# Attention and routing kernel: TensorE's fillers between the score products in another order

## The reference

```python
xl = _layer_norm(x, ln_l_g, ln_l_b);  xg = _layer_norm(x, ln_g_g, ln_g_b)
# x is (32, 256, 128), 16 heads of 8
...   # local: _mha over blocks of the first axis: all 32 rows see each other, per position
...   # glb: one _mha of xg with itself over the same 32 rows
return local + glb
...
x = _layernorm(x + attention(x))
logits = tokens @ Wg                      # 8 experts, capacity T / E
idx = jnp.argmax(gates, axis=1)           # one expert per token, places counted in token order
hidden = jax.nn.relu(jnp.einsum('ech,ehf->ecf', expert_in, W1) + b1[:, None, :])
expert_out = jnp.einsum('ecf,efh->ech', hidden, W2) + b2[:, None, :]
x = _layernorm(x + out)
```

## Time and profile before

| | us |
|---|---|
| median of 3 runs | 732.38 |
| lowest, highest | 731.19, 732.99 |
| span of the profiled execution | 731.2 |
| units 8 to 29, by GpSimd's step (168.00 to 486.48) | 318.5 |

### The profile page before, as it was taken

How to read it: one execution, slowest core, us unless ns; L and a number is a source line. 1 busy time by engine, 2 the same in 40 slices (tenths; PEclk the granted TensorE clock), 3 DMA queues, 4 the chain that set the end, 5 groups by cost and what they waited for, 6 DMA issues and landing times.

```text
span 731.2 us, 19237 instructions
## 1 busy us (share of the span) xinstructions
PE 637.1 (87%) x6502; PEld 358.2 (49%) x6502; DVE 549.3 (75%) x1652; ACT 489.6 (67%) x1108; POOL 488.8 (67%) x972
## 2 busy tenths in 40 slices
PE   0569698899999999999999999999999359999990
PEld 0435443454445444544555554455444237677770
DVE  5565596889998998899999998988993205666663
ACT  1425475887988888889888888898888233444430
POOL 4133333568888788888888887886776714667676
PEclk9857898999999999999999999999999569999996
DMA  5585589897576675575666765655631022333410
GB/s 111 142 169 110 145 202 174 211 179 211 154 138 170 161 128 148 129 167 158 120 168 162 140 156 151 129 152 111 155 64 36 24 64 81 98 107 99 123 47 32
DMA packets 144001, 95.53 MB, mean 131 GB/s; under 512 B 12052, under 2 KB 136173, under 8 KB 143904
## 3 DMA queue, kind: packets, MB, share of 16 engines
q1 hardware_dynamic: 138048, 85.54, 50.1%
q0 software_dynamic: 4096, 7.81, 3.8%
q10 hardware_dynamic: 1760, 0.96, 0.6%
HBM read 47.70 MB, written 45.74 MB: 128 GB/s over the span
## 4 chain that ended last, share of the span: by engine, by line
PE 49%; DVE 18%; DMA 9%; issue 8%; POOL 7%; SPq 6%; ACT 3%; POOLq 0%; ACTq 0%; DVEq 0%
DVE mx L940 10%; PE ps_o L555 10%; PE ps_b L528 7%; PE ps_a L1372 6%; PE ps_a L510 4%; PE ps_b L1366 3%; DMA ks<-k_stack 3%; DMA qs<-mT 3%; PE ps_m L586 2%; PE ps_f L476 2%; POOL out L1486 2%; PE ps_f L466 2%; PE ps_m L599 2%; SPq L326 2%; PE ps_f L471 2%
## 5 line engine op out<-in xcount | busy, mean ns | idle before, releaser
L940 DVE TENSOR_REDUCE mx<-ps_a 128x2 f32<-128x512 f32 (+1 forms) x576 | 359.9, 651 | 61.5 <-PE ps_a L510 59.6
L762 ACT ACTIVATE prob<-ps_b 128x512 f32<-128x512 f32 (+1 forms) x576 | 298.7, 572 | 75.8 <-PE ps_b L528 74.3
L528 PE MATMUL ps_b<-qs,ks 59*128 59x256 bf16 (+1 forms) x1152 | 192.5, 271 | 14.0 <-DMA qs<-mT 6.3
L510 PE MATMUL ps_a<-ks,qs 56*128 56x256 bf16 (+1 forms) x1152 | 190.0, 275 | 14.7 <-DMA ks<-k_stack 12.7
L555 PE MATMUL ps_o<-prob,vp 128*32 128x256 f32 (+1 forms) x2304 | 172.8, 384 | 0.4 <-ACT prob L762 0.4
L528 PEld LDWEIGHTS ps_b<-qs,ks 59*128 59x128 bf16 x1152 | 80.9, 96 | 106.7 <-ACT prob L762 52.0
L510 PEld LDWEIGHTS ps_a<-ks,qs 56*128 56x128 bf16 x1152 | 75.9, 96 | 27.8 <-DMA ks<-k_stack 14.4
L1486 POOL DMA_INDIRECT out<-res,dest x64 | 65.4, 1022 | 34.2 <-DVE res L1461 19.1
L1225 POOL DMA_INDIRECT routed<-row,slot x64 | 67.2, 1050 | 29.8 <-issue 26.3
L555 PEld LDWEIGHTS ps_o<-prob,vp 128*32 128x32 f32 x2304 | 49.8, 110 | 58.2 <-issue 50.2
L1159 POOL CAST mpart<-mx 128x16 bf16<-128x16 f32 x72 | 14.0, 195 | 70.8 <-DVE mx L940 60.0
(11 more groups left out here) (130 smaller groups left out, 1041.7 us busy)
## 6 DMA issues: line engine op xcount, KB each, us to landing
qs<-q_stack SPq DMA_DIRECT2D x72, 192.0 KB
ks<-k_stack SPq DMA_DIRECT2D x72, 192.0 KB
q_stack<-part SPq DMA_DIRECT2D x18, 384.0 KB
k_stack<-part SPq DMA_DIRECT2D x18, 384.0 KB
q_stack<-part SPq DMA_DIRECT2D x18, 256.0 KB
k_stack<-part SPq DMA_DIRECT2D x18, 256.0 KB
routed<-empty SPq DMA_DIRECT2D x8, 520.0 KB, 8.3
rows_sb<-routed SPq DMA_DIRECT2D x16, 260.0 KB, 3.7
```

What stands on the lines that cost most here:

```text
L510: ins = nc.tensor.matmul(ps_a[:, n % 3, qt * S:qt * S + keys.stop - keys.start], qs[half, b, hp, qt * P:(qt + 1) * P], ks[half, b, hp, key ...
L528: ins = nc.tensor.matmul(ps_b[:, 1 - e, kt * n:(kt + 1) * n], ks[half, u % 3, hp, kt * P:(kt + 1) * P], qs[half, u % 3, hp, queries], star ...
L762: nc.scalar.activation(prob[:, hp, half * n:(half + 1) * n], ps_b[:, half, 0:n], ACT.Exp).then_inc(exp_done, 1)
L940: nc.vector.reduce_max(mx[:, u % 2, :, col], ps_a[:, n % 3].rearrange("p (t k) -> p t k", t=2)[:, :, 0:k], axis=AX).then_inc(max_done, 1)
```

## The change

TensorE's fillers are dealt out anew: a value product does both key halves in one go (`values(u, q)`, eight products in a row) and these stand alone in slots 1, 3, 5 and 7; everything else stands in slots 0, 2, 4 and 6. Waits move with what they guard. The other engines' orders are fitted to it. The counts of the routing move to the last 24 columns of `ps_m`, so that they don't share columns with the turned maxima. The orders of GpSimd and SyncE stay as they are, row by row.

```diff
+        def values(u, q):
+            if there(u):
+                p_v(u, q, 0)
+                p_v(u, q, 1)
 
         def fill(u, hp):
             if hp == 0:
-                if there(u - 1):
-                    p_v(u - 1, 3, 0)
                 if there(u):
                     pe.wait_ge(mT_ready, 2 * u + 1)
...
                     turn_max(u, 1)
-            if hp == 1:
-                if there(u - 1):
-                    p_v(u - 1, 3, 1)
-                if routes(u - 3):
...
-                    count_tokens(u - 3)
                 if first is not None:
                     turn_x(first, 0)
                     turn_x(first, 1)
+                if second is not None:
+                    project_in(second, "k", 0)
+                    project_in(second, "k", 1)
+            if hp == 1:
+                values(u - 1, 3)
             if hp == 2:
+                if there(u):
+                    pe.wait_ge(mT_ready, 2 * u + 2)
...
+                if routes(u - 3):
+                    count_tokens(u - 3)
+                if first is not None:
+                    project_in(first, "q", 0)
                 if second is not None:
                     project_in(second, "v", 0)
-                    project_in(second, "v", 1)
...
                     turn_o(u - 1)
             if hp == 3:
-                if there(u):
-                    p_v(u, 0, 0)
+                values(u, 0)
+            if hp == 4:
+                if there(u - 1):
+                    pe.wait_ge(o_normed, u)
...
                 if there(u + 1):
...
                     turn_max(u + 1, 0)
                 if first is not None:
-                    project_in(first, "q", 0)
-            if hp == 4:
-                if there(u):
-                    p_v(u, 0, 1)
...
+                    project_in(first, "q", 1)
+                if second is not None:
+                    project_in(second, "v", 1)
+                if there(u + 1) and there(u - 1):
                     pe.wait_ge(mT_ready, 2 * u + 3)
...
+                if routes(u - 2):
+                    turn_x1(u - 2)
                 if there(u - 1):
                     turn_oN(u - 1)
...
             if hp == 5:
-                if there(u):
-                    p_v(u, 1, 0)
+                values(u, 1)
+            if hp == 6:
                 if routes(u - 2):
                     logits(u - 2)
                 if there(u - 1):
                     project(u - 1)
-            if hp == 6 and there(u):
-                p_v(u, 1, 1)
-                p_v(u, 2, 0)
             if hp == 7:
-                if there(u):
-                    p_v(u, 2, 1)
-                if first is not None:
-                    project_in(first, "k", 0)
-                    project_in(first, "k", 1)
+                values(u, 2)
...
         # ScalarE, step(u)
             if there(u):
-                exponential(u, 4)
+                exponential(u, 4, (0,))
+            if there(u + 1):
+                copy_max(u + 1, 0)
+            if there(u):
+                exponential(u, 4, (1,))
             if there(u - 1) or routes(u - 2):
                 copy_turned(u)
             if first is not None:
                 first_part_q(first)
             if second is not None:
+                place_v(second, 0)
                 place_v(second, 1)
...
         # VectorE, fill(u, hp, e)
             if at == (0, 0) and routes(u - 3):
-                top_priority(u - 3)
-            if at == (0, 1) and routes(u - 3):
+                priorities(u - 3)
+            if at == (0, 1):
+                if routes(u - 2):
+                    mean_variance(u - 2)
+                if routes(u - 3):
+                    top_priority(u - 3)
...
-            if at == (6, 1):
+            if at == (7, 0):
                 if there(u - 1):
                     add_residual(u - 1)
                 if routes(u - 2):
                     logit_max(u - 2)
-            if at == (7, 0):
+            if at == (7, 1):
                 if routes(u - 2):
                     shift_logits(u - 2)
                 if routes(u - 1):
                     statistics(u - 1)
-            if at == (7, 1):
-                if routes(u - 2):
-                    priorities(u - 2)
-                if routes(u - 1):
-                    mean_variance(u - 1)
```

More of the change, by code:

```diff
@@ L605, in count_tokens @@
             pe.wait_ge(mask_ready, batch(u) + 1)
-            nc.tensor.matmul(ps_m[:, 0:2 * E], c["tri_bf"][:], mask[:].rearrange("p t e -> p (t e)"), start=True, stop=False)
-            nc.tensor.matmul(ps_m[:, E:2 * E], c["ones_bf"][:], mask[:, 0], start=False, stop=True)
-            nc.tensor.matmul(ps_m[:, 2 * E:3 * E], c["ones_bf"][:], mask[:, 0], start=True, stop=False)
-            nc.tensor.matmul(ps_m[:, 2 * E:3 * E], c["ones_bf"][:], mask[:, 1], start=False, stop=True).then_inc(counted, 1)
+            at = 2 * S - 3 * E
+            nc.tensor.matmul(ps_m[:, at:at + 2 * E], c["tri_bf"][:], mask[:].rearrange("p t e -> p (t e)"), start=True, stop=False)
+            nc.tensor.matmul(ps_m[:, at + E:at + 2 * E], c["ones_bf"][:], mask[:, 0], start=False, stop=True)
+            nc.tensor.matmul(ps_m[:, at + 2 * E:at + 3 * E], c["ones_bf"][:], mask[:, 0], start=True, stop=False)
+            nc.tensor.matmul(ps_m[:, at + 2 * E:at + 3 * E], c["ones_bf"][:], mask[:, 1], start=False, stop=True).then_inc(counted, 1)
+        def values(u, q):
+            if there(u):
+                p_v(u, q, 0)
+                p_v(u, q, 1)
         def fill(u, hp):
@@ L755, in copy_bv, with exponential @@
             nc.scalar.copy(bv_col[:], ps_m[:, 0:2 * D]).then_inc(bv_col_ready, 1)
-        def exponential(u, hp):
+        def exponential(u, hp, halves=(0, 1)):
             wait(act, pv_done, 4 * u + hp // 2 - 3)
             n = 2 * (P if is_local(u) else S)
-            for half in range(2):
+            for half in halves:
                 act.wait_ge(scores, 16 * u + 2 * hp + half + 1)
@@ L812, in copy_counts @@
             wait(act, place_chain.sem, place_chain.steps * g)
-            nc.scalar.copy(count[:].rearrange("p a e -> p (a e)"), ps_m[:, 0:3 * E]).then_inc(counts_copied, 1)
+            nc.scalar.copy(count[:].rearrange("p a e -> p (a e)"), ps_m[:, 2 * S - 3 * E:2 * S]).then_inc(counts_copied, 1)
         def step(u):
@@ L819, in step @@
                 copy_max(u, 1)
+            if first is not None:
+                scale_shift(first)
             if second is not None:
@@ L823, in step @@
                 exponential(u, 1)
+            if there(u - 1):
+                copy_o(u - 1)
             if routes(u - 3):
                 copy_counts(u - 3)
-            if there(u - 1):
-                copy_o(u - 1)
             if there(u):
                 exponential(u, 2)
-            if first is not None:
-                scale_shift(first)
             if second is not None:
@@ L835, in step @@
                 exponential(u, 3)
-            if there(u + 1):
-                copy_max(u + 1, 0)
-            if second is not None:
-                place_v(second, 0)
             if routes(u - 2) and batch(u - 2) >= 3:
@@ L1043, in fill @@
                     input_stats(late, (2, 3))
+                if routes(u - 3):
+                    gate(u - 3)
             if at == (3, 0):
```

26 lines of the change are left out of this document (8 added, 18 removed).

## The result

The kernel became slower: 743.06 us (741.28 to 747.6, four runs) against 731.79 for the kernel before, ratio 1.0148 with an interval of 1.0111 to 1.0185. The forecast was 731.6, no difference, with a range of 724 to 739. The profiled execution took 739.5 us where the one before took 731.2.

What follows compares the result with a forecast made beforehand. GpSimd's 28.67 us of work per pair was taken as the bound. The profiled 731.2 - 1.2 (steady stage) + 1.0 (first stage) - 0.6 (last units) gave 730.4, a median of 731.6, range 724 to 739.

Steps and rivals of the forecast that it cites:

- Case B: Rival: GpSimd isn't the bound, its work has unseen slack and the whole 1.0 us per pair comes through; 715.5 us, chance 0.10.
- Fewer changes of form, -0.6: TensorE: merged value products mean fewer switches between scores, narrow and full array forms, saving about 0.6 us per pair.
- the wait for the output, -0.9: TensorE: with the turn of the maxima in slot 4, its wait for the normalised output goes, saving 0.9 us per pair.
- ScalarE in slot 4, +0.5: Odd units' value copies and the copy of the maxima delay ScalarE's exponentials, costing TensorE 0.5 us per pair (0 to 0.8).
- The moved mean and variance, +1.9: Steady stage: GpSimd's step starts later, so the stack load sets about half the pairs, costing 1.9 us over the stage.
- the sign that the prediction named: GpSimd idling over 0.5 us ahead of L1183 in most steps would show the moved mean and variance as the bound.
- the loop: GpSimd step to store, load, slot 6 and the step two units on: 57.05 to 58.6 us against 57.34 of GpSimd work.
- The first stage, +1.0: To 168 us: late mean and variance and held-back stores against faster slots, net loss 1.0 us (gain 1 to loss 3).
- The last units, -0.6: Last six units, from 486.48 us: no input to normalise, so GpSimd has room; a gain of 0.6 us.
- C: Rival: slower by the loop through the late mean and variance, 29.2 us per pair; 738.5 us, chance 0.28.
- D: The forecast itself: the change does what it says but is covered, no difference; 731.6 us (730.2 to 734.6), chance 0.36.

Runs made afterwards that it cites:

- e1: The changed kernel with the mean and variance of unit u-1 back in slot 7 of its unit; 735.78 us, ratio 1.008 to the kernel before.
- e9: The kernel before with part of GpSimd's work left out (input tiles, third part of k, row tiles); ratio 0.9952 to the kernel before.
- e19: The changed kernel with mean and variance back in slot 7 and the turn of the next unit's first maxima back in slot 3; 730.86 us, ratio 0.9999.
- e12: The changed kernel with part of GpSimd's work left out, mean and variance back in slot 7 and the turn of the maxima back in slot 3; ratio 0.9893.
- e3: The changed kernel with both value projection halves back in slot 2 of odd units and two value copies ahead of slot 4's exponentials; ratio 1.0151.
- e10: The changed kernel with part of GpSimd's work left out and mean and variance back in slot 7; ratio 1.001 to the kernel before.
- e2: The kernel before with the mean and variance moved to slot 0 of the next unit, as in the changed kernel; ratio 1.0179.

## Why the prediction was wrong, point by point

*The step that failed* is the price of the moved mean and variance. I put 1.9 us on it over the steady stage, and nothing for the half clock behind a late load. With it the stage takes 325.0 us, without it (e1) 316.7: 8.3 us, and by the ratios 0.7 to 1.1%, 5 to 8 us. The second fault is the turn of the maxima a slot later, which I let the faster slots of the first stage all but pay for: it is worth 0.4 to 0.8%, 3 to 6 us.

*What bounds the kernel.* I read 28.77 us as 28.67 of GpSimd's work and 0.1 of wait. This was wrong in both parts: GpSimd has 28.5 (e1), and the kernel before takes 28.77 with part of it left out too (e9). GpSimd followed the other engines 0.3 us a pair below its own limit. Case B, that GpSimd isn't the bound, was thus right about the old kernel, but its result, 715.5, needed GpSimd to stay out of the way at 27.8, and it doesn't: e19, whose other engines need 27.8, falls back to GpSimd's 28.5. The Trainium skill's page Perfetto Trace Analysis, section Identifying the Most-Contended Engine, would name VectorE there as well; the trace of e19 doesn't agree: from 340 to 400 us VectorE is 94% busy and GpSimd 85%, and the pace is GpSimd's.

*Fewer changes of form, -0.6, and the wait for the output, -0.9.* Together 1.5 were expected, and 1.0 came: e12 has 27.8 where the old order has 28.8. How it splits between the two no run shows. The wait did vanish, but also in e12, where the turn is still in slot 3. What removed it was the other order of the fillers, not the moved turn.

*ScalarE in slot 4, +0.5.* The size was right and the cause was not. The value copies cost nothing (e3); what costs 0.5 goes with the turn and its copy between the exponentials. With this the three engines need 28.3 and not 27.8. That left, under GpSimd's 28.5, a gain of 0.2 to 0.3 per pair, 3 us in all.

*The moved mean and variance, +1.9.* The mechanism was right: TensorE waits in slot 6 of even units for a load that hangs on GpSimd's late step. GpSimd's step 18 began 1.17 us behind exponential 0 of its unit (318.87 against 317.70), before 0.34 (313.24 against 312.90): 0.8 later, where my sum has 1.0. (The text beside it says from 1.0 to 1.6 us into the unit, which doesn't fit that sum.) GpSimd idled 0.3 to 1.3 us ahead of the steps of the steady stage that it had no backlog for. That is the sign that the prediction named, over 0.5 us in most steps, in 15 of 27. What I had wrong is the price, and in the loop it is the last term. From step to store the change takes 24.4 to 25.3 us (I had 24.55), from store to slot 6 13.3 to 15.0 (13.5 to 15.07), but from slot 6 to the GpSimd step two units on 19.4 to 19.7 where I had 19.0, and 20.8 to 20.9 in the three places where the half clock lies in it. Nothing stands in the sum for that half clock; with their waits these three units took 7.2 us more. And half the pairs at up to 1.3 us each would allow 7 us; the text doesn't say how 1.9 comes out of it. So the steady stage lost 6.5 us instead of gaining 1.2.

*The first stage, +1.0.* Measured 1.9 (exponential 0 of unit 8 at 168.94 after 167.09), within the bounds that I gave. The stores that wait behind the placing of the maxima were the right mechanism. In unit 5 they start when they did before, though GpSimd has the third part ready 2.5 us earlier (129.22 after 131.73):

```profile
126.95 2.27 POOL L1144 TENSOR_TENSOR part<-rest,part 128x512 bf16<-128x512 f32 x2 [0.70 <-ACT part L732]
...
130.57 1.47 SPq L378 DMA_DIRECT2D qs<-mT  x2
132.09 1.49 SPq L326 DMA_DIRECT2D q_stack<-part  x3
```

What the faster slots had won was held back there. The turn's place is worth 3.3 us by unit 8 (e1 over e19), and with less work on GpSimd 5.6 by unit 8 and 9.9 by unit 10 (e10 over e12); a part of these two is the half clock that e10 meets at 144.4 and at 181.9 us.

*The last units, -0.6:* measured +0.3 behind unit 30.

*The rivals.* The kernel ended beyond C's 738.5, by C's mechanism and by what C doesn't have, the turn and the clock; 0.28 was too little for a loop whose length I had myself put at or above the pair. D's claim, that the new order of the fillers is merely covered, isn't shown by the 0.9999 of e19 without the two moved steps: there the gain was made and lost again in two units with a late load and a half clock.

## What to carry to other kernels

An engine that shows the same interval in every step may only follow. Cut its work and see whether the interval moves before it is called the bound. A wait of TensorE on a late load can have a half clock behind it, here 1.1 us of wait and 1.3 of half clock in three units, and so the margin of a load can be worth more than the idle time that it prevents. Before a result is produced a slot later, look at what stands behind its transfer on an in-order queue, and on ScalarE try a small copy where the engine waits, rather than between two passes that feed TensorE.

## What the runs showed of the hardware

The granted clock fell to 0.50 for 3.4 us (in e2, e3 and e12 also for 6.8 or 10.2) behind waits of TensorE, and then came back to 1.0. The profiled executions have 3 such falls in the steady stage of the change, 2 in e19, none in the kernel before and in e1. Ahead of the three falls in the change, TensorE's longest pause was 0.90, 0.85 and 0.93 us. Not every such wait was followed by one: in the change the pauses of 1.35 us at 175.2 and of 1.04 us at 298.1 were not, and e2 has a pause of 0.9 us in every even unit of its steady stage and a whole clock from 180 us on. The kernel before has no pause between its matmuls over 0.4 us between 150 and 540 us. Which waits bring a fall, no run settles.

No version with all of its work done beat the kernel before; e12 would, at 0.989, but only with less work on GpSimd. So the next things to shorten are GpSimd's 28.5 us a pair and the way of the load, for which TensorE waits in e12 and e19 too.
